# Gelu of layers 2 and 3 written in place into its PSUM bank, which is held until the low part is subtracted; the order anew

## What is computed

```python
h = silu(x @ w1.T * w1_s) * (x @ w2.T * w2_s)      # 128 -> 512, called layer 1
h = gelu(h @ h1.T * h1_s)                           # 512 -> 512, layer 2
h = gelu(h @ h2.T * h2_s)                           # 512 -> 512, layer 3
out = h @ w3.T * w3_s                               # 512 -> 128, layer 4
x = x + 0.5 * out                                   # x enters the block normalised over its features
```

## Time and profile before

| what | value |
|---|---|
| device time, median of 3 runs | 367.62 us (367.56 to 367.99) |
| span of the profiled execution | 366.2 us |
| PE busy | 359.0 us (98%) |
| DVE busy | 319.5 us (87%) |
| ACT busy | 283.6 us (77%) |
| POOL busy | 171.9 us (47%) |

### The profile page before, as it was taken

The page is one execution under the profiler, slowest core; times in us unless marked ns, Lnnn a source line. Parts: engine busy times, 40 slices in busy tenths (PEclk is TensorE's granted clock), DMA queues, the critical chain, the costliest instruction groups (busy, mean ns, idle before and its releaser), DMA issues.

```text
span 366.2 us, 5192 instructions
## 1 busy us (share of the span) xinstructions
PE 359.0 (98%) x1572; PEld 284.6 (78%) x1572; DVE 319.5 (87%) x542; ACT 283.6 (77%) x463; POOL 171.9 (47%) x259
## 2 busy tenths in 40 slices
PE   7999999999999999999999999999999999999995
PEld 2678888778877887887878787887878877888885
DVE  5999788989989989999999989999999799947742
ACT  5898777886897789777876969868888796777763
POOL 3583375694124578512794545663574740520000
PEclk9999999999999999999999999999999999999999
DMA  7725504042000302100221021022024010050001
...
DMA packets 17534, 21.44 MB, mean 59 GB/s; under 512 B 7392, under 2 KB 8672, under 8 KB 17248
## 3 DMA queue, kind: packets, MB, share of 16 engines
...
...
## 4 chain that ended last, share of the span: by engine, by line
PE 97%; DVE 1%; ACT 0%; issue 0%; POOL 0%; POOLq 0%; DVEq 0%
PE hid_ps L654 62%; PE gate_ps L654 8%; PE y_ps L654 8%; PE up_ps L654 7%; PE y_ps L673 2%; PE xt_ps L847 2%; PE xt_ps L843 2%; PE xt_ps L850 2%; PE y_ps L763 1%; PE up_ps L718 1%; PE gate_ps L718 1%; DVE full L1092 0%; PE xt_ps L654 0%; DVE gate L1080 0%; DVE xt_sb L1152 0%
## 5 line engine op out<-in xcount | busy, mean ns | idle before, releaser
L654 PE MATMUL hid_ps<-act_hi,hi_h 128*128 128x512 f32 (+1 forms) x368 | 146.5, 398 | 0.0
L654 PE MATMUL hid_ps<-act_lo,hi_h 128*128 128x512 f32 (+1 forms) x368 | 143.1, 389 | 0.0
L1102 DVE TENSOR_TENSOR act_lo<-full,act_hi 128x512 fp32r<-128x512 f32 x157 | 117.3, 769 | 20.9 <-ACT act_hi L918 17.7
L911 ACT ACTIVATE full<-hid_ps,vec 128x512 f32<-128x512 f32 x123 | 84.3, 686 | 53.3 <-PE hid_ps L654 36.9
L654 PEld LDWEIGHTS hid_ps<-act_lo,hi_h 128*128 128x128 f32 x368 | 69.2, 188 | 16.3 <-issue 1.4
L654 PEld LDWEIGHTS hid_ps<-act_hi,hi_h 128*128 128x128 f32 x368 | 69.2, 188 | 16.0 <-issue 1.4
L918 ACT ACTIVATE act_hi<-full 128x512 fp32r<-128x512 f32 x127 | 78.6, 628 | 1.6
L580 POOL TENSOR_TENSOR xnt<-xt_sb,wide 128x512 f32<-128x512 f32 x22 | 31.6, 1437 | 49.5 <-DMA wide<-rows 43.8
L654 PE MATMUL hid_ps<-act_hi_second,hi_h 128*128 128x512 f32 x128 | 52.1, 407 | 0.0
L654 PE MATMUL hid_ps<-act_lo_second,hi_h 128*128 128x512 f32 x128 | 50.0, 390 | 0.0
L894 ACT ACTIVATE tanh<-gate_ps,s_half 128x512 f32<-128x512 f32 x60 | 40.6, 682 | 8.9 <-PE gate_ps L654 8.8
...
## 6 DMA issues: line engine op xcount, KB each, us to landing
...
```

Of the source, the lines that this page charges most:

```text
L654: mm = eng.matmul(ps, w, a, start=(first and n == 0), stop=(last and n == len(seq_) - 1))
L911: eng.activation(full23[m % 2][:, :], home23(n, T, m)[:, :], ACT.Gelu, scale=col("sh1" if n == 2 else "sh2", m)).then_inc(s_gelu[n], 1)
L1102: eng.tensor_tensor(act_lo[a][:, m, :], full[m % 2][:, :], act_hi[a][:, m, :].bitcast(F32), ALU.subtract).then_inc(s_lo[n], 1)
```

## The change

The gelu of layers 2 and 3 no longer writes to the SBUF tile but back into the bank it reads (for tile 0 it still writes `full23`). The high part is copied from the bank, and the low part is subtracted from there. So PE may start on the bank only when the low part of the chunk two back is done, and the gelu has no wait for a low part any more. `p23` waits for `s_lo` where it waited for `s_gelu`. The tables of all engines are written anew, for the start too.

```diff
+        def gelu_out(n, T, m):
+            return home23(n, T, m) if T > 0 else full23[m % 2]
...
                 elif n == 2 and m < 2:
-                    eng.wait_ge(s_gelu[3], MC * T - MC + m + 3)
+                    eng.wait_ge((s_lo if T > 1 else s_gelu)[3], MC * T - MC + m + 3)
...
                 elif n == 3 and m < 2:
-                    eng.wait_ge(s_gelu[2], MC * T + m + 3)
+                    eng.wait_ge(s_lo[2], MC * T + m + 3)
                 else:
-                    eng.wait_ge(s_gelu[n], MC * T + m - 1)
+                    eng.wait_ge((s_lo if T > 0 else s_gelu)[n], MC * T + m - 1)
...
                 if h == 0:
-                    eng.wait_ge(s_gelu[3], MC * T + MC - 2)
+                    eng.wait_ge(s_lo[3], MC * T + MC - 2)
...
             def gelu(n, T, m):
                 eng.wait_ge(s_p[n], MC * T + m + 1)
-                if n == 2 and m < 2:
-                    if T > 0:
-                        eng.wait_ge(s_lo[3], MC * T - MC + m + 3)
-                elif n == 3 and m < 2:
-                    eng.wait_ge(s_lo[2], MC * T + m + 3)
-                else:
-                    eng.wait_ge(s_lo[n], MC * T + m - 1)
-                eng.activation(full23[m % 2][:, :], home23(n, T, m)[:, :], ACT.Gelu,
+                if T == 0 and m >= 2:
+                    eng.wait_ge(s_lo[n], m - 1)
+                elif (n, T) == (3, 0):
+                    eng.wait_ge(s_lo[2], m + 3)
+                eng.activation(gelu_out(n, T, m)[:, :], home23(n, T, m)[:, :], ACT.Gelu,
...
-                eng.activation(act_hi[n][:, m, :], full23[m % 2][:, :], ACT.Copy).then_inc(s_hi[n], 1)
+                eng.activation(act_hi[n][:, m, :], gelu_out(n, T, m)[:, :], ACT.Copy).then_inc(s_hi[n], 1)
...
-                full = full1 if n == 1 else full23
+                full = full1[m % 2] if n == 1 else gelu_out(n, T, m)
...
     "ACT": (
-        "hi:w1 bits:w2 hi:w2 z vec:s1 0:t bits:h1.1 bits:h1.3 0:tanh.0 0:tanh.1 0:tanh.2 0:high1.0 0:high1.1",
+        "bits:w2",
+        "0:z hi:w1 hi:w2 t bits:h1.1 vec:s1 tanh.0 tanh.1 bits:h1.3 tanh.2 high1.0 high1.1 tanh.3 bits:h2.0 "
...
     "PE": (
-        "p2.0 p2.1 p2.2 p2.3 p1.0 p1.1 p4 p1.2 p3.0 p3.1 p1.3 p3.2 p3.3",
-        "p2.0 p2.1 p2.2 p2.3 p4 p3.0 p3.1 p3.2 last:p4a last:p3.0 last:p3.1 last:p4b last:p4c.0 last:p4c.1",
+        "13:p2.2 13:p2.3 15:u 14:p1.3 13:p3.0 13:p3.1 13:p3.2 13:p3.3 p2.0 p2.1 p4 p1.0 p1.1 p2.2 p2.3 p1.2 "
+        "p1.3 p3.0 p3.1 p3.2 p3.3 15:p2.0 15:p2.1",
+        "p2.2 p2.3 p4 p3.0 p3.1 p3.2 last:p4a last:p3.0 last:p3.1 last:p4b last:p4c.0 last:p4c.1",
```

More of the change, by code:

```diff
@@ L32 @@
     "ACT": (
-        "hi:w1 bits:w2 hi:w2 z vec:s1 0:t bits:h1.1 bits:h1.3 0:tanh.0 0:tanh.1 0:tanh.2 0:high1.0 0:high1.1",
-        "bits:h2.0 bits:w3 tanh.3 high1.2 z.0 z.1 high1.3",
[4 rows of a table added]
     ),
     "DVE": (
[5 rows of a table removed]
+        "stats",
[6 rows of a table added]
     ),
@@ L52 @@
     "SP": (
[L53 to L67, removed]
@@ L68 @@
-        "store",
+        "park wide 3:park 3:wide",
+        "a0:park a0:wide 4:park 4:wide a1:park 5:park a1:wide 5:wide 6:park 6:wide",
+        "a2:park 7:park a2:wide 7:wide",
+        "a3:park 8:park a3:wide 8:wide 9:park",
+        "9:wide a4:park 10:park",
+        "a4:wide 10:wide",
+        "",
+        "",
+        "a5:park 11:park a5:wide 11:wide 8:store",
+        "12:park 12:wide",
+        "store a6:park a6:wide 13:park a7:park 13:wide a7:wide 14:park 10:store 11:store",
+        "14:wide",
@@ L69 @@
+        "",
+        "park",
+        "15:wide",
+        "12:store 13:store store",
     ),
     "POOL": (
[L71 to L78, removed]
@@ L79 @@
-        "norm a4:xn.0 a4:xn.1 xn.0 xn.1",
-        "a3:dt a5:norm a4:weight a5:xn.0 a5:xn.1 norm a4:dt xn.0 xn.1",
-        "norm a5:weight xn.0 xn.1",
-        "a6:norm a6:xn.0 a6:xn.1 a5:dt norm a6:weight a7:norm xn.0 xn.1",
-        "a6:dt a7:xn.0 a7:xn.1 norm xn.0 xn.1",
-        "a7:weight a7:dt norm xn.0 xn.1",
-        "",
-        "",
+        "hi:h2.0 hi:h2.1 hi:h2.2 norm 3:norm hi:h2.3 xn.0 xn.1",
+        "hi:w3 xn.0 xn.1 a0:norm 4:norm a0:xn.0 a0:xn.1 4:xn.0 4:xn.1 a1:norm 5:norm a0:weight a1:xn.0 "
@@ new lines @@
+        "a1:xn.1 5:xn.0 5:xn.1 6:norm",
+        "a0:dt",
+        "",
+        "",
+        "6:xn.0 6:xn.1 a2:norm norm a2:xn.0 a2:xn.1 xn.0 xn.1 a1:weight a3:norm 8:norm",
+        "a1:dt a2:weight a3:xn.0 a3:xn.1 xn.0 xn.1",
+        "norm a2:dt a4:norm xn.0 xn.1 a3:weight",
+        "",
+        "",
+        "10:norm a4:xn.0 a4:xn.1 10:xn.0 10:xn.1 a3:dt a5:norm 11:norm a4:weight a5:xn.0 a5:xn.1 11:xn.0 "
+        "11:xn.1 a4:dt norm xn.0 xn.1 a5:weight a6:norm a6:xn.0 a5:dt a6:xn.1 13:norm a7:norm a6:weight "
@@ L87 @@
+        "13:xn.0 13:xn.1 a7:xn.0 a7:xn.1 a6:dt",
+        "14:norm a7:weight 14:xn.0 14:xn.1 a7:dt 15:norm",
+        "",
+        "",
+        "",
+        "15:xn.0 15:xn.1",
     ),
     "PE": (
[17 rows of a table removed]
[22 rows of a table added]
     ),
     "ACT": (
[41 rows of a table removed]
[39 rows of a table added]
     ),
     "DVE": (
[35 rows of a table removed]
[39 rows of a table added]
     ),
@@ L926, in last_gelu @@
                 eng.wait_ge(s_last_p3, h + 1)
-                if h == 0:
-                    eng.wait_ge(s_lo[3], MC * T + MC - 2)
                 eng.activation(halves(full23[(MC - 1) % 2], h), last_hid[h], ACT.Gelu,
@@ L1099, in low @@
                     eng.wait_ge(s_lo[1], m)
-                full = full1 if n == 1 else full23
+                full = full1[m % 2] if n == 1 else gelu_out(n, T, m)
                 a = first_act(T) if n == 1 else n
-                eng.tensor_tensor(act_lo[a][:, m, :], full[m % 2][:, :], act_hi[a][:, m, :].bitcast(F32),
+                eng.tensor_tensor(act_lo[a][:, m, :], full[:, :], act_hi[a][:, m, :].bitcast(F32),
                                   ALU.subtract).then_inc(s_lo[n], 1)
```

## The result

The changed kernel takes 377.66 us (median of 4 runs, 376.13 to 379.33); the kernel before took 367.81 on the same chip. The ratio is 1.026, with a 95% interval of 1.0225 to 1.0295: slower by 9.9 us. The forecast of 374.1 us was 3.6 us too low, inside its range. The profiled execution is the one of 376.13 us, with a span of 374.3 us against 366.2, so the trace explains 8.1 us and not all of the median's 9.9.

A forecast was written before the change was run, and what follows sets the result against it. PE was taken to bound the kernel, at its pitch from about 26 to 358 us. Tail 3.2, middle 3.0 and start 0.3 added 6.5 to the 366.2 us span; with 1.4 for the median, 374.1 us; 8-in-10 range 369.0 to 383.0.

The forecast's parts named there:

- The pair rule: Between two chunks on one PSUM bank, PE needs 0.65 us of other work besides one chunk, or waits for the rest.
- the tail: Tiles 13 to 15: six pairs of chunks with no other work between cost PE 3.2 us, between 2.5 and 3.9.
- The restart rule: The gelu starts 0.43 us after a chunk's last matmul starts; PE restarts 0.18 us after the low part ends.
- Rival 2: Gelu in place is slow, 0.6 us more each, as ACT reads and writes one bank: 388 us at least; chance 0.05.
- The start: First 26 us: roundings of w1 and w2 behind `z` delay the first product; +0.3 us, between -0.5 and +0.9.
- The middle: Tiles 2 to 13: 18 places with one p1 or attention product of other work cost 3.0 us, between 0 and 14.
- tight places: The 24 places where the held bank may make PE wait: the six pairs and 18 from tile 2 to 13.
- None of the three moves the end: Removed gelu wait (15.8 us), cheaper high parts (6 us of ACT), fewer low-part outliers (up to 11 us of DVE): costed at 0.
- Rival 1: Tiles 2 to 13 become a chain of waits: the gelu's 15.8 us pass to PE, 386.6 us; chance 0.11.
- Rivals 3 and 4: No change, the hold costs nothing, 367.4 to 368.3 us, chance 0.08; faster, the start decides, 366.7 us, chance 0.08.

The follow-up runs named there:

- little POOL: POOL's four kinds of 128x512 SBUF instructions done on 128 of 512 columns: in the changed kernel 373.40 us, in the changed orders without the held bank 371.35 us.

## Why the prediction was right, and where it was off

**The pair rule and the tail** held by measurement. Forecast: six pairs at 0.58 us in six named places, 3.2 us net. Measured: six in those places, 3.35 us, 3.3 net. The restart rule (0.43 us to the gelu, 0.18 behind the low part) held: the low part of the pair shown ends 2.02 us behind the gelu's start, and the restart is worth 0.16 us later.

**ACT and DVE durations.** Forecast for the high part 577 ns, measured 599; for the gelu 640 to 690, measured 660; for the low part 680 with few outliers, measured 685 with none. Rival 2, a slow gelu in place, is excluded. The low part's median is 691 ns from PSUM and was 685 from SBUF. The Trainium skill's 125 against 60 ns for DVE (Perfetto Trace Analysis, Optimizing Scalar/DVE Operations) would have made 65 ns of it: the measurement says 6.

**The start** cost 0.7 us in the trace and not 0.3. The first product came at 8.67, sooner than the 8.85 forecast, and the first tanh at 9.88, sooner than before. But the roundings ahead of `xn_hi` put DVE's `xn_lo` later (8.56, before 8.12) and with it the stats and the first gate; ACT's look at the weights behind the second tanh put the flag's sum (`inexact`) behind both gates; and the flag's copy stands behind both `up`. Before:

```profile
9.87 0.87 DVE L1051 BATCH_NORM_STATS2 stats<-x_sb 128x6 f32<-128x128 f32 x4
10.66 0.14 DVE L1033 TENSOR_REDUCE inexact<-bits 128x1 f32<-128x6 f32 x1
10.72 1.29 DVE L1080 SCALAR_TENSOR_TENSOR gate<-tanh,gate_ps 128x512 f32<-128x512 f32 x2
...
12.59 0.14 DVE L1038 CAST flag_i<-gate_ps 1x1 int32<-1x1 f32 x1
```

After:

```profile
10.20 0.86 DVE L1063 BATCH_NORM_STATS2 stats<-x_sb 128x6 f32<-128x128 f32 x4
10.98 1.26 DVE L1092 SCALAR_TENSOR_TENSOR gate<-tanh,gate_ps 128x512 f32<-128x512 f32 x2
12.16 0.15 DVE L1045 TENSOR_REDUCE inexact<-bits 128x1 f32<-128x6 f32 x1
12.23 1.40 DVE L1104 SCALAR_TENSOR_TENSOR full<-up_ps,s_half,gate 128x512 f32<-128x512 f32 x2
13.55 0.14 DVE L1050 CAST flag_i<-gate_ps 1x1 int32<-1x1 f32 x1
```

The flag is copied 0.96 us later, where 0.1 to 0.3 were forecast, and PE restarted at 14.37 us and not 13.48.

**The middle** is the term that was mis-sized: 3.0 us forecast, 4.7 in the trace, and most of the 1.5 us by which the median lies above the profiled run is likely here too (not shown by a trace, but the runs of the changed kernel spread over 3.2 us, and with little POOL over 0.7 and 0.4). The step that failed: the working took DVE's outliers for a relief only ("if they come from its two SBUF operands the change saves DVE up to 120 x 0.09 = 11 us") and priced the tight places by gate, up, the reciprocal and the exp. It overlooked that 70 of the 189 low parts (62 of layer 1, 8 of tile 0) keep two SBUF operands and stand in the same queue, and that POOL's `xnt` reaches PE through ACT. One such place:

```profile
302.05 1.29 POOL L597 TENSOR_TENSOR xnt<-xt_sb,wide 128x512 f32<-128x512 f32 x1 [0.56 <-DMA wide<-rows]
302.39 1.50 DVE L1114 TENSOR_TENSOR act_lo_second<-full,act_hi_second 128x512 fp32r<-128x512 f32 x1
...
303.82 0.68 DVE L1114 TENSOR_TENSOR act_lo<-hid_ps,act_hi 128x512 fp32r<-128x512 f32 x1
...
304.55 0.50 PE L671 MATMUL hid_ps<-act_hi,hi_h 128*128 128x512 f32 x1 [0.52 <-DVE act_lo L1114]
```

A layer-1 low part, stretched to 1.50 us behind POOL, holds up the low part that frees the bank. The little-POOL run puts 3.4 us on POOL's work, such meetings and late `xnt` together, and 1.4 on the rest, in which the instructions that the forecast had named lie. The mechanism, an instruction ahead of the low part on DVE, was right; which instruction it would be was not. The forecast took 3.0 us for the named ones by a third of a bound, at least twice what they cost, and nothing for POOL; that the two errors partly cancel is luck, and part of why the total lies so near.

**The premise that "None of the three moves the end"** is true of the old orders and false of the new ones. There the relief of DVE and POOL from each other is worth more than everything that the hold costs: without both, the same orders take 394 us. What this leaves open is a bank not held and a low part from PSUM at once, which needs another bank. It wasn't tried.

**Rival 1**, a chain of waits, did not come with the new tables, and the old tables show what it looks like: 444 us. **Rivals 3 and 4**, no change and a gain by the start, are excluded by the time, 2.25 to 2.95% above the kernel before; the start was later and not sooner.
